# Second attention of a vision tower: projection or join before the transposes, values one step late

## The reference, cut to what matters

```
for e in range(4):
    q, k, v = x @ wq[e].T, x @ wk[e].T, x @ wv[e].T       # 12 heads of 16
    attn = softmax(where(causal, q k / sqrt(16), -1e30))
    outs.append((attn @ v) @ wo[e].T)
fused = concatenate(outs)                                  # 4 * 192
return silu(fused @ w_gate.T) * (fused @ w_up.T)
```

## Time and profile before

| | |
|---|---|
| median of 3 runs | 411.57 us (411.3 to 412.5) |
| the profiled execution | 411.31 us, its span 409.6 us |
| mean granted clock of TensorE | 0.982 |
| TensorE busy in the span | 384.5 us (94%) |
| VectorE | 250.9 us (61%) |
| ScalarE | 174.7 us (43%) |
| GpSimd | 45.6 us (11%) |
| chain that ended last | PE 73%, DVE 15%, ACT 5% |

### The profile page before, as it was taken

How to read it: one execution, slowest core, us unless ns; L and a number is a source line. 1 busy time by engine, 2 the same in 40 slices (tenths; PEclk the granted TensorE clock), 3 DMA queues, 4 the chain that set the end, 5 groups by cost and what they waited for, 6 DMA issues and landing times.

```text
span 409.6 us, 8771 instructions
## 1 busy us (share of the span) xinstructions
PE 384.5 (94%) x3602; PEld 315.0 (77%) x3602; DVE 250.9 (61%) x728; ACT 174.7 (43%) x304; POOL 45.6 (11%) x97
## 2 busy tenths in 40 slices
PE   8999999999877899999999989999999999999993
PEld 8988878788554657565548788998999899879783
DVE  1567766603497988888444487558458206677344
ACT  1256551842455565755435635235224310551420
POOL 7130010330000000100001400000000200304003
PEclk9999999999978999999999999999999989989999
DMA  7999500000289100000003996224401000000001
GB/s 194 258 223 252 118 9 2 2 0 0 61 229 272 53 2 2 2 2 3 2 0 87 280 265 162 77 60 134 130 9 56 2 0 2 2 2 2 0 2 38
DMA packets 28725, 30.69 MB, mean 75 GB/s; under 512 B 4867, under 2 KB 24137, under 8 KB 28686
## 3 DMA queue, kind: packets, MB, share of 16 engines
q1 hardware_dynamic: 28220, 29.96, 29.1%
q10 hardware_dynamic: 306, 0.17, 0.2%
q0 software_dynamic: 160, 0.01, 0.0%
HBM read 29.73 MB, written 0.39 MB: 74 GB/s over the span
## 4 chain that ended last, share of the span: by engine, by line
PE 73%; DVE 15%; ACT 5%; issue 2%; DMA 2%; POOL 2%; SPq 0%; DVEq 0%; POOLq 0%
PE ps L1510 66%; PE ps L1514 6%; DMA front<-in_x 2%; DVE front L1170 2%; DVE front L1171 2%; PE ps L1522 2%; DVE front L1179 1%; DVE front L1181 1%; DVE front L1164 1%; DVE bn L1015 1%; POOL rstd L524 1%; ACT front L745 1%; DVE front L1166 1%; DVE xn L1030 1%; DVE mv L1018 0%
## 5 line engine op out<-in xcount | busy, mean ns | idle before, releaser
L1510 PE MATMUL ps<-halves 128*128 128x512 f32 (+2 forms) x380 | 84.1, 376 | 1.3 <-ACT front L732 1.3
L1510 PEld LDWEIGHTS ps<-halves 128*128 128x128 f32 x380 | 66.5, 188 | 13.4 <-ACT front L732 1.7
L1510 PE MATMUL ps<-wide,front 128*128 128x192 f32 x432 | 73.7, 332 | 0.0
L1510 PEld LDWEIGHTS ps<-wide,front 128*128 128x128 f32 x432 | 72.0, 194 | 1.0 <-issue 0.5
L1510 PEld LDWEIGHTS ps<-front 64*32 64x32 f32 (+3 forms) x1488 | 52.0, 134 | 21.8 <-issue 9.4
L1510 PE MATMUL ps<-front 64*32 64x64 f32 (+3 forms) x1488 | 60.7, 245 | 8.1 <-ACT front L745 3.0
L732 ACT ACTIVATE front<-ps,colc 128x512 f32<-128x512 f32 x60 | 39.6, 690 | 52.3 <-PE ps L1510 52.2
L1313 DVE SCALAR_TENSOR_TENSOR xn<-ps,small,xn 128x192 f32<-128x192 f32 x28 | 9.7, 410 | 29.7 <-PE ps L1510 29.7
L1514 PE MATMUL ps<-ident,front 128*128 128x128 f32 x144 | 21.5, 286 | 6.5 <-DVE front L1181 5.3
L1514 PEld LDWEIGHTS ps<-ident,front 128*128 128x128 f32 x144 | 16.2, 144 | 10.2 <-DVE front L1181 7.2
L1510 PE MATMUL ps<-xT,turned 128*64 128x256 f32 (+1 forms) x96 | 23.4, 482 | 0.0
(11 more groups left out here) (280 smaller groups left out, 555.5 us busy)
## 6 DMA issues: line engine op xcount, KB each, us to landing
wide<-in_w SPq DMA_DIRECT2D x8, 576.0 KB, 4.7
wide<-in_w SPq DMA_DIRECT2D x8, 384.0 KB, 5.8
wide<-in_w SPq DMA_DIRECT2D x16, 192.0 KB, 6.3
front<-in_a2w SPq DMA_DIRECT2D x5, 576.0 KB
front<-in_a1w SPq DMA_DIRECT2D x5, 384.0 KB
front<-in_x SPq DMA_DIRECT2D x3, 512.0 KB, 7.9
front<-in_w_qkv SPq DMA_DIRECT2D x2, 576.0 KB, 7.7
front<-in_a1w SPq DMA_DIRECT2D x5, 192.0 KB
```

What stands on the lines that cost most here:

```text
L1510: return pe.matmul(o, l, r, start=start, stop=stop)
```

## The change

On TensorE the piece of a step (projection, values_in, join or gate_up) stands before `turn1(n)` instead of behind it, and `values1(n - 1)` stands where `values1(n)` stood; the last one follows the loop. The pieces are dealt out anew. Before: step t = 0 projections 0 and 1 of the next expert, t = 1 projection 2, t = 2 the join of the expert before, t = 3 values_in. After: t = 0 projection 2 of the next expert; expert 0: values_in(1) in step 1, the projections 0 and 1 of expert 2 in steps 2 and 3; expert 1: the join in step 1, values_in(2) in step 2, projections 0 and 1 of expert 3 in step 3; expert 2: the join in step 1, values_in(3) by halves in steps 2 and 3; expert 3: nothing in step 0, the join in step 1, two gate_ups each in steps 2 and 3. Ahead of the loop `scores1(1)` moves before `values_in(0, 1)`. On ScalarE the first eviction of a step and `exp1(n + 2)` stand before `pT1_out(n)`, `oT_out(n - 1)` takes the place of `oT_out(n)`, and `fT_out` follows it.

```diff
 # ScalarE
             for n in range(N1):
                 e, t = divmod(n, NT)
-                pT1_out(n)
-                if e < EA - 1:
-                    if t == 0 and e >= 1:
-                        qk_out(e + 1, 0)
-                    elif t == 1:
-                        qk_out(e + 1, 2)
-                    elif t == 3:
-                        v_out(e + 1, 0)
+                if t == 0 and e < EA - 1:
+                    qk_out(e + 1, 2)
+                elif e == 0 and t == 1 or e == 1 and t == 2:
+                    v_out(e + 1, 0)
+                elif e == EA - 2 and t >= 2:
+                    v_out(e + 1, t - 2)
+                elif e == 0 and t >= 2:
+                    qk_out(2, t - 2)
+                elif e == 1 and t == 3:
+                    qk_out(3, 0)
                 if n + 2 < N1:
                     exp1(n + 2)
+                pT1_out(n)
+                if e == 0 and t == 1 or e == 1 and t == 2:
+                    v_out(e + 1, 1)
+                elif e == 1 and t == 3:
+                    qk_out(3, 1)
                 if 4 <= n < 4 + PAIRS:
                     fade_out(n - 4)
-                if e < EA - 1:
-                    if t == 0 and e >= 1:
-                        qk_out(e + 1, 1)
-                    elif t == 3:
-                        v_out(e + 1, 1)
-                if e >= 1 and t == (2 if e < EA - 1 else 0):
+                if n >= 1:
+                    oT_out(n - 1)
+                if e >= 1 and t == 1:
                     fT_out(e - 1)
-                oT_out(n)
                 if e == EA - 1 and t >= 2:
...
                     w1_high(t - 2)
+            oT_out(N1 - 1)
 # TensorE
             scores1(0)
             values_in(0, 0)
+            scores1(1)
             values_in(0, 1)
-            scores1(1)
...
                 if n + 2 < N1:
                     scores1(n + 2)
-                turn1(n)
-                if e < EA - 1:
-                    if t == 0 and e >= 1:
-                        project1(e + 1, 0)
-                        project1(e + 1, 1)
-                    elif t == 1:
-                        project1(e + 1, 2)
-                    elif t == 2 and e >= 1:
-                        join(e - 1, 0)
-                        join(e - 1, 1)
-                    elif t == 3:
-                        values_in(e + 1, 0)
-                        values_in(e + 1, 1)
-                elif t == 0:
+                if t == 0 and e < EA - 1:
+                    project1(e + 1, 2)
+                elif e == 0 and t == 1 or e == 1 and t == 2:
+                    values_in(e + 1, 0)
+                    values_in(e + 1, 1)
+                elif e == 0:
+                    project1(2, t - 2)
+                elif t == 1:
                     join(e - 1, 0)
                     join(e - 1, 1)
-                elif t < 3:
+                elif e == 1:
+                    project1(3, 0)
+                    project1(3, 1)
+                elif e == EA - 2:
+                    values_in(e + 1, t - 2)
+                elif t == 2:
                     pe.wait_ge(s["fT_top"], EA - 1)
                     pe.wait_ge(s["fT_end"], EA - 1)
-                    gate_up(t + 1, first)
-                else:
+                    gate_up(2, first)
+                    gate_up(3, first)
+                elif t == 3:
                     pe.wait_ge(s["s1_read"], N1)
                     gate_up(0, first)
-                values1(n)
-
-            gate_up(1, first)
+                    gate_up(1, first)
+                turn1(n)
+                if n >= 1:
+                    values1(n - 1)
+            values1(N1 - 1)
             join(EA - 1, 0)
             join(EA - 1, 1)
```

## The result

The changed kernel takes 420.81 us in the median of 4 runs (418.07 to 421.86), beside 411.73 before: a ratio of 1.0211, 95% interval 1.0169 to 1.0253. Four further runs in a later comparison gave 416.15 to 421.00, ratio 1.0114 (1.0051 to 1.0178). Both intervals lie above 1: it is slower, by 5 to 9 us, where 2.5 were forecast. A ratio leaves out runs that lie over 1.5% above the fastest of their kernel, a median doesn't, so the ratio is what to compare.

A forecast was written before the change was run, and what follows sets the result against it. TensorE and VectorE were taken as near their limits, the order of waits deciding. New waits of 16.68 us less 13.9 of old holes and half clock gave +2.8, taken as +2.5: 414.1 us, range 411.9 to 416.7.

The forecast's parts named there:

- the term for the clock: TensorE's granted clock in the second attention stage: 1.00 from 116 to 213, the old half-clock stretch of 2.75 us gone.
- The sum, 16.68 - 13.9: Second attention stage: 16.68 us of new waits less 13.9 of old holes and half clock, +2.8, taken as +2.5.
- rival (A): TensorE's clock falls: old half-clock stretch stays or a new one opens at a hole; 415.7 or 416.2 to 416.9; chance 0.30.
- The sentence on the Trainium skill: Rule against the change: by the skill the clock falls in one of the new holes at join(0), turn(12) or join(2).
- The waits: Twelve new TensorE waits in the stage, most for ScalarE copies queued behind exp1, 0.32 to 2.82 us each, 16.68 in all.
- What would show it: Signs: holes of 2 to 3 us before join(0) and join(2) ended by L788, smaller ones by L776 or L780, clock 1.00.
- (a): TensorE's waits for pT1 evictions before values go, holes like that of 0.90 us in steps without a piece.
- (b): Three TensorE holes of 1.0 us at qk_out(e+1,2) go, since project1(e+1,2) runs a step earlier.
- (c): TensorE's hole of 1.97 us and smaller ones at the softmax go in part, as two first-expert steps gain projections.
- Rival (B): Faster: ScalarE does not hold the joins, waits there vanish, -6.1 us, so 405.5; chance 0.12 with its halves.
- Rival (C): VectorE is the bound and the order of TensorE's work is indifferent: 411.3 to 411.8 us; chance 0.05.
- (d): The slow start of the stage goes: TensorE's half clock at 120 to 122, 2.75 us, stays at full level.

The follow-up runs named there:

- e1: Changed kernel with spare products filling TensorE's holes before join(0), join(1), join(2), turn(12) and the gate_ups of step 14; 414.78 us, ratio 1.0058.
- e5: The changed kernel run again with no edit, for more runs and a second profile; 417.90 us, ratio 1.0114.
- e4: Kernel before the change, with 3, 3 and 6 spare products before turn(0), values(0) and turn(1); 411.29 us, ratio 1.0016.
- e2: Changed kernel with ScalarE's list in input order: evictions, fT_out, pT1_out, oT_out, then exp1 and fade, second w1_high behind the last oT_out; 407.53 us, ratio 0.9898.
- e9: Changed kernel with exp1 and the fade moved behind oT_out on ScalarE, fT_out still last, 6 spare products before turn(12); 415.77 us, ratio 1.0031.
- e3: e2 with 9 spare products before turn(12); 404.44 us, ratio 0.9846.
- e6: Changed kernel with 8 spare products before join(0) and nowhere else; 417.39 us, ratio 1.0080.
- e8: Projections, joins and values_in in their steps of before (third join in step 13), still ahead of the transposes, ScalarE as in e2; 407.15 us, ratio 0.9865.
- e7: e3 with gate_up(0) between values(14) and values(15) and gate_up(1) between values(15) and join(3); 405.62 us, ratio 0.9808.
- e10: e8 with 9 spare products before turn(2); 406.53 us, ratio 0.9864.

## Why the prediction was wrong

**Where it failed.** The step that failed is the term for the clock. The sum, 16.68 - 13.9, priced every new wait at its length and had the clock at 1.00 from 116 to 213: what the holes do to the clock behind them was put at nothing. The runs show 6.1 us for it in the first profile and 8.5 in the second (e1, e5), against 2.9 of waits. The prediction had the fall as rival (A), once, at 2.1 to 2.75 us, with a chance of 0.30; it came twice in both profiles, at 3.0 to 4.5 us a time. Two mistakes lie in this. The rows at half clock were of shorter groups, and 2.75 was carried to a place where the next group is a join of 3.85 us that goes to 6.1 or 7.4. And one hole of 1.97 that had left the clock up was weighed as evidence, when the same hole was followed by a fall in e4. The sentence on the Trainium skill named the right thing: "TensorE: Matmul & The Clock Gate", section "HAM oscillation — how this bites in real kernels", has pauses between bursts bring the clock down again and again; with more than one long hole, more than one fall was to be reckoned, and the traces agree (144 to 148 and 192 to 196 at 0.50). The page's example has longer pauses, for DMAs; that holes of 2.3 and 2.4 us can do it is what these traces add.

**What held.** The waits: forecast 105.8 us for the stage at full clock (89.1 + 16.68), measured 105.84 (e1). The place and releaser of each: L788 before the joins, L780 before values_in and gate_up, as "What would show it" had them. The cause, exp1 ahead of pT1_out and oT_out on an engine that takes its list in order: e2 removes the holes by ScalarE's list alone, e9 those at the joins by moving exp1 and the fade. (a), (b) and (c) are real: TensorE's idle time in the stage that L800 ended went from 1.8 to 0 us, at L745 from 3.0 to 0.5, at the softmax from 5.3 to 2.1. With ScalarE's order mended and turn(12) filled the same TensorE list is 6.0 us shorter than before (e3), where -6.1 was given as the bound with those waits gone; without the spare products it is 4.3 (e2).

**Rival (B)** lost as a forecast of this change, and was right as a price: 405.5 us against 404.44 in e3. **Rival (C)** is out: VectorE's last softmax ended at 196.19 - 106.28 = 89.9 us after the first scores, 0.7 us sooner than the 90.6 of before, and the stage is 9 us longer. That end was forecast some 4 us sooner, which failed with the clock: the wait of 4.33 behind join(0) was to be 1.13.

**(d)**, the gain of a full clock at the start, was seen (1.00 from 116 to 141). By itself it shows only in e4, as 1.7 us up to turn(3), before the next fall took it.

## What to carry to other kernels

When work is moved on one engine, write out the lists of the engines that feed it: an instruction that itself waits (here an exponential, for VectorE's softmax) holds every copy behind it, so copies that others wait for go ahead of it. And price a new hole on TensorE not by its length alone but also by what stands behind it, at the half clock: 3.0 to 4.5 us where that was a join, nothing where another wait took it up, and for each such hole. In every profile with spare products the clock stayed up at the holes that they filled; at holes left open it fell in e4, e6 and e9.

## What the runs showed of the hardware

- Behind the same hole the clock fell to its half level in some executions and not in others: turn(12) with 1.91 us (full in the first profile of the changed kernel, fallen in e5 and e6), turn(3) with 1.97 (full before, fallen in e4). It fell behind holes of 2.33 to 2.69 too (changed kernel, e2, e5, e8, e9). Length alone doesn't decide: it fell behind 0.79 and 0.90 before, and in e9 behind 0.59 and 0.93, holes that the changed kernel has as well without a fall.
- The fall can come late, in the work behind the hole: the clock was 1.00 until 142, when join(0) had run since 141.00. In e8 it was down at once (0.52 from 127 to 128, where the hole ended at 127.05). How long it stays down varies between executions of one kernel, some 7 us in the first profile and 10 and 14 in e5.
- The clock also fell with TensorE busy for 6.00 of 6.00 us (e7, 324 to 330, 0.72). The Trainium skill, "TensorE: Matmul & The Clock Gate", section "What's actually happening", explains the low level by a lack of activity. Taken as the busy time of the profile, this row disagrees; but what TensorE did just before were products over 8 and 3 rows, in all six profiles with this fall. Whether it is these that bring it, no run tested, and in six others they did not.
- TensorE pauses of 0.3 to 1.1 us inside values1 without a releaser ("issue") came and went between kernels (0.33 in e3, 0.83 and 0.78 in e7, 1.07 in e10). Their cause is open, and they can hide a gain of their size, as in e10.
